# A graph network and a mixture of experts on one core: the experts' router turned round, and the gates' small operations spread over three engines

## The reference, cut to what matters

```
logits = xf @ Wr + br                    # 10000 x 8, xf = layernorm(x)
probs = softmax(logits); vals, idx = top_k(probs, 2)
cw = (one_hot(idx, 8) * vals[..., None]).sum(axis=1)
for e in range(8):                       # W1e 512 x 64, W2e 64 x 512
    h = relu(xf @ W1e + b1e)
    out += cw[:, e:e+1] * (h @ W2e + b2e)
x = x + out
```

## Time and profile before

| | |
|---|---|
| median of 3 runs | 2534.85 us |
| all runs | 2534.85, 2533.58, 3272.83 us |
| profiled execution, its own time | 2537.42 us |
| its span | 2535.6 us |
| mean granted clock of the profiled execution | 0.998 |
| busy over the span | PE 98%, DVE 74%, ACT 59%, POOL 44% |

### The profile page before, as it was taken

The page is one execution under the profiler, slowest core; times in us unless marked ns, Lnnn a source line. Parts: engine busy times, 40 slices in busy tenths (PEclk is TensorE's granted clock), DMA queues, the critical chain, the costliest instruction groups (busy, mean ns, idle before and its releaser), DMA issues.

```text
span 2535.6 us, 40119 instructions
## 1 busy us (share of the span) xinstructions
PE 2492.7 (98%) x9827; PEld 1624.6 (64%) x9827; DVE 1874.8 (74%) x4816; ACT 1491.9 (59%) x3550; POOL 1106.9 (44%) x1451
## 2 busy tenths in 40 slices
PE   8999999999999999999999999999999999999999
PEld 4444455555488874555558886555546888888887
DVE  5555565555599985555579996557748999999997
ACT  2222245555288875555548886555535666666665
POOL 3222245555144435555433333555534544444452
PEclk9999999999999999999999999999999999999999
DMA  5444468888355547888735555998852334533332
GB/s 149 133 133 133 130 201 265 272 266 271 96 166 165 163 162 254 273 263 273 248 96 166 164 165 188 337 335 271 271 184 80 103 106 137 168 117 93 105 102 70
DMA packets 208171, 460.89 MB, mean 182 GB/s; under 512 B 34896, under 2 KB 35208, under 8 KB 208005
## 3 DMA queue, kind: packets, MB, share of 16 engines
q0 software_dynamic: 64928, 207.55, 29.3%
q1 hardware_dynamic: 73812, 125.17, 14.1%
q10 hardware_dynamic: 69264, 126.12, 13.6%
HBM read 245.32 MB, written 213.93 MB: 181 GB/s over the span
## 4 chain that ended last, share of the span: by engine, by line
PE 79%; DVE 14%; issue 3%; DMA 1%; ACT 1%; POOL 0%; ACTq 0%; SPq 0%; DVEq 0%; POOLq 0%
PE psY L695 11%; PE psM L809 9%; PE psY L809 9%; PE psH L809 9%; PE psY L709 6%; PE psY L717 6%; PE psY L726 6%; PE psT L675 5%; PE psS L821 4%; PE psS L822 4%; DVE xls L1466 1%; DVE res L1554 1%; DVE res L1540 1%; DVE xcs L1469 1%; DVE rows L1530 1%
## 5 line engine op out<-in xcount | busy, mean ns | idle before, releaser
L566 POOL DMA_INDIRECT rows<-y_rows,lists x471 | 491.7, 1044 | 461.8 <-PE psS L822 339.8
L1359 DVE TENSOR_TENSOR lows<-rows,highs 128x512 fp32r<-128x512 f32 x471 | 325.8, 692 | 356.7 <-ACT highs L977 348.3
L977 ACT ACTIVATE outs<-psS 128x512 f32<-128x512 f32 x471 | 279.6, 594 | 272.2 <-PE psS L822 267.2
L977 ACT ACTIVATE highs<-rows 128x512 fp32r<-128x512 f32 x471 | 294.8, 626 | 147.2 <-ACT outs L977 107.1
L821 PE MATMUL psS<-highs,sel 128*128 128x512 f32 x471 | 346.9, 737 | 10.3 <-ACT outs L977 8.0
L573 POOL DMA_INDIRECT rows<-sum_rows,nodeI x158 | 211.2, 1337 | 313.8 <-DVE rows L1367 298.9
L695 PE MATMUL psY<-wy,res 128*128 128x512 f32 x632 | 286.7, 597 | 0.0
L977 ACT ACTIVATE outs<-psY 128x512 f32<-128x512 f32 x237 | 141.7, 599 | 231.2 <-PE psY L695 221.8
L809 PE MATMUL psM<-wz,res 128*128 128x512 f32 x544 | 255.6, 592 | 0.0
L809 PE MATMUL psY<-wz,res 128*128 128x512 f32 x536 | 251.7, 592 | 0.0
L809 PE MATMUL psH<-wz,res 128*128 128x512 f32 x528 | 248.0, 592 | 0.0
(11 more groups left out here) (201 smaller groups left out, 4893.2 us busy)
## 6 DMA issues: line engine op xcount, KB each, us to landing
sum_rows<-outs ACTq DMA_DIRECT2D x471, 256.0 KB, 3.7
y_rows<-outs SPq DMA_DIRECT2D x237, 256.0 KB, 2.0
rows<-in_x POOLq DMA_DIRECT2D x78, 256.0 KB, 3.2
outs<-in_x SPq DMA_DIRECT2D x78, 256.0 KB
out_rows<-res SPq DMA_DIRECT2D x78, 256.0 KB, 2.9
rows<-y_rows,lists POOLq DMA_INDIRECT x471, 4.3
z_rows<-res SPq DMA_DIRECT2D x13, 512.0 KB, 5.6
res<-z_rows SPq DMA_DIRECT2D x13, 512.0 KB, 4.5
```

The lines of the kernel that those rows point to most:

```text
L566: pool.indirect_dma_start(out=rows[:, t % RING, :], out_offset=None, in_=y_d, in_offset=bass.IndirectOffsetOnAxis(ap=col(srcT, t), axis=0) ...
L977: act.activation(o, i_, ACT.Copy).then_inc(signal, 1)
L1359: dve.tensor_tensor(lows[:, t % RING, :], rows[:, t % RING, :], highs[:, g, :].bitcast(F32), ALU.subtract)\
```

## The change

Five things change, all in the experts' stage.

1. The router's product is turned round: `wg2` (16 columns) is the stationary operand, and high and low part of the tile, now one tensor `x_both`, stream past together as 256 columns. Four matmuls take the place of eight, and the result is 16 x 256 in psM.
2. To have the logits by node again, ACT copies and negates that result to `logitT` (`take_logits`), and PE turns it with two 128 x 128 transposes after `up_parts` (`router_turn`).
3. DVE sums the four parts in one reduction over psM, ahead of `up_wide`; the bias's subtraction and the minimum stand each in front of a 512-column operation instead of waiting for one another.
4. The gates' high part goes from DVE to ACT (`gates_high`, behind `gated`), the low part from DVE to POOL (`gates_low`, first in POOL's iteration).
5. On POOL `scale_shift` stands ahead of `gather_own`. Some pairs of semaphores become one.

```diff
@@ POOL @@
+            def gates_low(k):
+                s = k % 2
+                high, low = (sm[:, s, a:a + 2 * X].rearrange("p (g e) -> p g e", g=2) for a in (HIGH, LOW))
+                pool.wait_ge(cw_high, k + 1)
+                pool.tensor_tensor(low, sm[:, s, CW:CW + X].unsqueeze(1).to_broadcast([P, 2, X]), high,
+                                   ALU.subtract).then_inc(cw_set[s], 1)
...
             for k in range(NT):
+                if k >= 1:
+                    gates_low(k - 1)
                 if k + 2 < NT:
                     negative_mean(k + 2)
                 gates(k)
+                if k + 2 < NT:
+                    scale_shift(k + 2)
                 if k + 4 < NT:
                     gather_own(k + 4, var_in, 1)
-                if k + 2 < NT:
-                    scale_shift(k + 2)
+            gates_low(NT - 1)
@@ PE @@
             def router(k):
...
+                pe.wait_ge(logit_set, k)
+                for q in range(C):
+                    mm = pe.matmul(psM[0:2 * X, 0:2 * P], wg2[:, q, :], x_both[:, :, s, q * P:(q + 1) * P],
+                                   start=(q == 0), stop=(q == C - 1))
+                mm.then_inc(router_ps, 1)
+
+            def router_turn(k):
+                s = k % 2
+                pe.wait_ge(logit_set, k + 1)
                 if k > 0:
                     pe.wait_ge(lg_sb[1 - s], (k - 1) // 2 + 1)
-                for q in range(C):
-                    pe.matmul(psM[:, 0:2 * X], xhs[:, s, q * P:(q + 1) * P], wg2[:, q, :], start=(q == 0), stop=False)
-                for q in range(C):
-                    mm = pe.matmul(psM[:, 0:2 * X], xls[:, s, q * P:(q + 1) * P], wg2[:, q, :], start=False,
-                                   stop=(q == C - 1))
-                mm.then_inc(lg_ps[s], 1)
+                for j in range(2):
+                    mm = pe.transpose(psM[:, (2 + j) * P:(3 + j) * P], logitT[:, j * P:(j + 1) * P], ident[:, :])
+                mm.then_inc(lg_ps, 1)
@@ ACT @@
+            def take_logits(k):
+                s, n = k % 2, k // 2
+                act.wait_ge(router_ps, k + 1)
+                act.wait_ge(lg_ps, k)
+                act.activation(logitT[0:2 * X, :], psM[0:2 * X, 0:2 * P], ACT.Copy, scale=-1.0).then_inc(logit_set, 1)
...
+            def gates_high(k):
+                s, n = k % 2, k // 2
+                act.wait_ge(cw_made, k + 1)
+                if k > 1:
+                    act.wait_ge(cw_ps, k - 1)
+                act.activation(sm[:, s, HIGH:HIGH + 2 * X].rearrange("p (g e) -> p g e", g=2).bitcast(F32R),
+                               sm[:, s, CW:CW + X].unsqueeze(1).to_broadcast([P, 2, X]), ACT.Copy).then_inc(cw_high, 1)
...
+                take_logits(k)
                 if k >= 1:
                     gated(k - 1)
+                    gates_high(k - 1)
@@ DVE @@
-                link(dve.tensor_copy(high.bitcast(F32R), twice))
-                dve.tensor_tensor(low, twice, high, ALU.subtract).then_inc(cw_set[s], 1)
...
                 if own:
+                    dve.wait_ge(lg_ps, k + 1)
+                    parts = psM[:, 2 * P:4 * P].rearrange("p (h r) -> p h r", h=2)[:, :, 0:2 * X]
+                    k_lg = step(dve.tensor_reduce(gate(LG), parts.rearrange("p h (g e) -> p e h g", g=2), AX.XY, ALU.add))
+                    up_wide(k)
                     after(k_lg)
-                    dve.tensor_reduce(stat(LOWEST), gate(LG), AX.X, ALU.min).then_inc(lg_sb[s], 1)
-                    up_wide(k)
+                    k_lg = step(dve.tensor_tensor(gate(LG), gate(LG), bgs[:, :], ALU.subtract))
```

More of the change, by code:

```diff
@@ L144, in build @@
         h_cross = nc.alloc_sbuf_tensor_at("h_cross", [P, D], F32R, offset=wz_at + 8 * D)
-        xhs = nc.alloc_sbuf_tensor_at("xhs", [P, 2, D], F32R, offset=wy_at)
-        xls = nc.alloc_sbuf_tensor_at("xls", [P, 2, D], F32R, offset=wy_at + 8 * D)
+        x_both = nc.alloc_sbuf_tensor_at("x_both", [P, 2, 2, D], F32R, offset=wy_at)
+        logitT = nc.alloc_sbuf_tensor_at("logitT", [P, 2 * P], F32, offset=wz_at + 12 * D)
+        xhs = x_both[:, 0]
+        xls = x_both[:, 1]
         xcs = nc.alloc_sbuf_tensor_at("xcs", [P, 2, D], F32R, offset=hw_at)
@@ L247, in build @@
         rstd_in = sems("rstd_in", 2)
-        shift_in = sems("shift_in", 2)
+        shift_in = sem("shift_in")
         oh_set = sems("oh_set", 4)
@@ L264, in build @@
         mend_st = sem("mend_st")
-        lg_ps = sems("lg_ps", 2)
+        lg_ps = sem("lg_ps")
         lg_sb = sems("lg_sb", 2)
-        p_sb = sems("p_sb", 2)
+        p_sb = sem("p_sb")
         cw_set = sems("cw_set", 2)
         hg_sb = sems("hg_sb", 2)
-        cw_ps = sems("cw_ps", 2)
+        cw_ps = sem("cw_ps")
+        cw_high = sem("cw_high")
         cw_sb = sems("cw_sb", 2)
@@ L288, in build @@
         pad_set = sem("pad_set")
+        router_ps = sem("router_ps")
+        logit_set = sem("logit_set")
         mean_in = sem("mean_in")
@@ L634, in scale_shift @@
                 pool.tensor_tensor(st[:, s, SHIFT:SHIFT + 1], st[:, s, MEAN:MEAN + 1], st[:, s, RSTD:RSTD + 1], ALU.mult)\
-                    .then_inc(shift_in[s], 1)
+                    .then_inc(shift_in, 1)
             def gates(k):
@@ L921, in hidden_turn @@
                 pe.transpose(psS[1][0:4 * X, 0:P], sm[:, s, HIGH:HIGH + 4 * X], ident[:, :])\
-                  .then_inc(cw_ps[s], 1)
+                  .then_inc(cw_ps, 1)
             def down_parts(k):
@@ L955, in _ @@
                 up_parts(k)
+                router_turn(k)
                 if k == 2:
@@ L1086, in exps @@
                                bias=st[:, s, LOWEST:LOWEST + 1], accum_out=st[:, s, SUM:SUM + 1])\
-                   .then_inc(p_sb[s], 1)
+                   .then_inc(p_sb, 1)
             def squares(k):
@@ L1104, in gated @@
                 g_.then_inc(hg_sb[s], 1)
+            def gates_high(k):
[5 more added lines that the diff above has]
+                               sm[:, s, CW:CW + X].unsqueeze(1).to_broadcast([P, 2, X]), ACT.Copy).then_inc(cw_high, 1)
             def norm(k):
                 s, n = k % 2, k // 2
-                act.wait_ge(shift_in[s], n + 1)
+                act.wait_ge(shift_in, k + 1)
                 act.activation(rows[:, 2 + s, :], kept(place(k)), ACT.Identity, scale=st[:, s, RSTD:RSTD + 1],
@@ L1117, in h_top @@
                 act.wait_ge(o_ps[s], n)
-                act.wait_ge(cw_ps[s], n + 1)
+                act.wait_ge(cw_ps, k + 1)
                 copy(cwT[0:4 * X, s, :], psS[1][0:4 * X, 0:P], cw_sb[s])
@@ L1145, in _ @@
             gated(NT - 1)
+            gates_high(NT - 1)
             widen_down(NT - 2)
@@ L1509, in gate @@
                     return sm[:, s, k:k + size]
[L1511 to L1516, removed]
                 if ahead:
@@ L1530, in experts @@
                     step(dve.scalar_tensor_tensor(v, a, 0.0, avec[:, :], ALU.min, ALU.mult))
+                if own:
+                    after(k_lg)
+                    dve.tensor_reduce(stat(LOWEST), gate(LG), AX.X, ALU.min).then_inc(lg_sb[s], 1)
+                if ahead:
                     dve.wait_ge(xe_in[s], 16 * (na + 1))
@@ L1533, in experts @@
                 if own:
-                    dve.wait_ge(p_sb[s], n + 1)
+                    dve.wait_ge(p_sb, k + 1)
                     step(dve.reciprocal(stat(INV), stat(SUM)))
@@ L1632, in _ @@
                     finish(k - 3)
-                if k >= 1:
-                    gate_parts(k - 1)
                 experts(k, ahead=(k + 2 < NT))
@@ L1639, in _ @@
             h_parts(NT - 2)
-            gate_parts(NT - 1)
             finish(NT - 2)
```

2 lines of the change are left out of this document (1 added, 1 removed).

## The result

The changed kernel takes 2517.78 us in the median (2517.22 to 2520.04, 5 runs). Its ratio to the kernel before is 0.9931, with a 95% interval of 0.9917 to 0.9946; run again later beside other kernels it was 0.9943 (0.9929 to 0.9957). The prediction said 2521 us, 0.55% faster, within 2513 to 2535. The interval does not reach 1, so the gain is clear of the noise, but it is under 2%, as the prediction had it with 0.96. The 3272.83 us among the runs of the kernel before is a slow execution; ratios compare fast ones alone.

A forecast was written before the change was run, and what follows sets the result against it. PE was taken to bound the kernel at 7.64 us an iteration, DVE next at 7.60. 76 x 0.18 us plus 0.5 once, less 0.2 in the drain, gave -14 us: median 2521 us, range 2513 to 2535.

The forecast's parts named there:

- PE led, by 0.04 us: Experts' stage before the change: PE sets the 7.64 us period, DVE alone needs about 7.60, read from its catching up early.
- PE's sum, -0.18 with ends -0.23 and +0.24: PE per iteration: old router -0.90, new router +0.50, two transposes +0.22 us, giving a period of 7.46 us.
- the margin around a stream: New router on PE: 0.017 us around each matmul's streaming time, so 0.124 us for 256 columns.
- DVE's need, 7.21: DVE per iteration after the change: 7.60 less 0.39 us for small operations removed or placed ahead of large ones.
- ACT and POOL hide what they are given: take_logits (0.35 us) and gates_high on ACT, gates_low (0.20 or twice that) on POOL: covered, costing nothing.
- The circle at 7.15 us: Logits' loop through PE, ACT and DVE back to the next router: 7.04 us, perhaps 0.1 more, under PE's 7.46.
- The reciprocal: DVE operation needing exps' sum: due 2.09 us after the reduction begins, just in time; otherwise some 0.1 us is added.
- -0.5 once for the late gather: POOL's moments ahead of the gather: norm no longer waits for a late gather, which once cost PE 0.5 us.
- The sum, -14 us: Whole profiled execution: 76 iterations at 0.18 us and 0.5 once, less 0.2 in the drain; 2537.4 to 2523.4 us.
- (a): Rival: the logits' circle or DVE leads at 7.46 to 7.64 us; 2521 to 2535 us; chance 0.19 together with (c).
- (b): Rival: new router's four matmuls charged as plain float32, 0.86 to 0.92 us; time 2553 us; chance 0.06.
- (c): Rival: PE gets its 0.18 but DVE keeps 7.60 us; 3 us gained, 2531; chance 0.19 together with (a).

The follow-up runs named there:

- e2: The kernel before with only the gates' split moved, high part to ACT and low part to POOL: 2535.02 us, ratio to before 0.9998.
- e5: The changed kernel with router_turn's two transposes made twice: 2536.51 us, ratio to before 1.0001.
- e6: The changed kernel with two of up_parts' four low matmuls left out: 2498.79 us, ratio to before 0.9854.
- e3: The changed kernel with the gates' split back on DVE: 2522.11 us, ratio to before 0.9942.
- e1: The kernel before with only POOL's order changed, scale_shift ahead of gather_own: 2536.09 us, ratio to before 0.9997.
- e4: The changed kernel with POOL's old order, the gather ahead of scale_shift: 2522.86 us, ratio to before 0.9946.
- e9: The changed kernel run again without any edit: 2520.13 us, ratio to before 0.9943.
- e7: The changed kernel with the bias's subtraction and the minimum directly behind the reduction, ahead of up_wide: 2521.24 us, ratio to before 0.9940.
- e8: The changed kernel with high and low part added in psum by eight 128-column router matmuls, leaving one transpose: 2516.36 us, ratio to before 0.9924.
- e11: The changed kernel with the activation's slope as one constant in experts' ahead part, a one-source DVE operation: 2519.18 us, one execution, no ratio.

## Why the prediction was right, point by point

**PE led, by 0.04 us.** That PE led is right: e2 takes work off DVE in the kernel before and gets nothing, and in the changed kernel e5 adds two transposes to PE and gets 0.233 us. The 0.04 rests on the one stretch of the prediction; no run tested it by itself.

**PE's sum, -0.18 with ends -0.23 and +0.24.** Measured -0.20. The transposes were 0.23 (0.22 taken) and the four wide matmuls 0.47 (0.50 taken), 0.117 each instead of 0.124, so that the old router's 0.90 closes the sum. The term that was mis-sized is the margin around a stream: I took 0.017 us from the 512-column group, and it is 0.010 with 16 columns of weights. The Trainium skill's rule ("TensorE: Matmul & The Clock Gate", "Back-to-back issue gap"), columns / 2.4 + 2.5 ns, gives 0.109; the page states it for a single matmul, without its weight load, which the prediction did not say. The trace's 0.117 lies between it and my value.

**DVE's need, 7.21.** Right: 7.207 in e6, and 7.50 in e3, which by the same sum would be 7.21 + 0.31 = 7.52.

**ACT and POOL hide what they are given.** Right for ACT: take_logits took 0.375 us (0.35 taken), gates_high 0.199 (0.20) and norm 0.802 (0.80), the turn's copy was there in time, and PE never waited. gates_low took 0.61 us where I had 0.20 to 0.40, and it is hidden all the same.

**The circle at 7.15 us.** Not seen, since DVE's 7.21 lies over it; e6 shows that it is not longer. The reciprocal did not wait.

**-0.5 once for the late gather.** 0.65, shown by e1 (gone) and e4 (back, 0.85). That POOL's order is worth another 0.025 us an iteration in the changed kernel I did not foresee.

**The sum, -14 us.** The profiles are 17.8 apart. Of the missing 3.8, 1.3 are the router's (75 x 0.200 against 13.7), 0.15 the late iteration, 0.5 the drain and the time ahead of the first router, which got shorter and not longer, and 1.8 the first three iterations, probably most of it the clock. The change itself is worth 15.5 to 16 us, by those executions and by the medians of e9 and of the kernel before beside it (2520.13 and 2536.22). So the mechanism was right and the size some 10% low.

**The rivals.** (a) fell with e6. (b), the price of plain float32, fell with 0.117 us a matmul. (c), DVE keeps 7.60, fell with e6 and e3 (its time, 2535 less 3, is 2532 and not 2531); but a part of the gain does hang on DVE's relief, as e3 shows.

## What to carry to other kernels

When two engines stand full, find out which leads from the stretches where one catches up, and count what the other needs alone: here they lay 0.04 us apart by that reading. DVE's relief alone gained nothing (e2), PE's relief with only a part of DVE's stopped at 7.50 us (e3), and the gates' move, worth nothing by itself, was worth 4 us together with the router. A product with few output columns is a candidate for having these columns as the stationary side, since the cost is then the columns streamed and not eight full weight loads, even if the result has to be turned back: here 0.47 and 0.23 us against 0.90. In a chain of small DVE operations each link costs 0.19 to 0.22 us (e7); placed singly in front of large ones with nothing to wait for, each costs 0.07 to 0.08.

## What the runs showed of the hardware that I had not expected

**The price of a matmul with 16 columns of weights.** Start to start: 0.117 us for 256 columns and 0.060 for 128, where 16 columns against 128 columns of weights cost 0.112. So the weight load of 128 columns sets the small ones' pace, and with 16 columns of weights it is gone.

**POOL and DVE exclude each other while DVE works on two operands in sbuf.** (psum is where PE leaves its products, sbuf the memory of the other tiles.) gates_low (128 x 16) takes 0.21 us in e2, where, in the timeline of both engines, it starts as L1532 has ended and ends before L1504, which reads psum, begins some 0.1 us later:

```profile
2207.11 0.75 DVE L1532 SCALAR_TENSOR_TENSOR rows<-rows,rdeg,res 128x512 f32<-128x512 f32 x1
...
2207.87 0.21 POOL L658 TENSOR_TENSOR sm<-sm 128x16 f32<-128x16 f32 x1
...
2208.17 0.70 DVE L1504 SCALAR_TENSOR_TENSOR psY<-psY,res 128x512 f32<-128x512 f32 x1 [0.24 <-PE psY L911]
```

In the changed kernel it starts at 2210.85 and ends at 2211.46, just behind L1558 (2210.70 to 2211.38), which reads rows and avec, both in sbuf. POOL's timeline of the changed kernel:

```profile
2208.67 0.19 POOL L639 TENSOR_TENSOR st<-st 128x1 f32<-128x1 f32 x1
2209.38 1.43 POOL L620 DMA_INDIRECT rows<-sum_rows,nodeI  x1 [0.52 <-issue]
2210.85 0.61 POOL L662 TENSOR_TENSOR sm<-sm 128x16 f32<-128x16 f32 x1
```

The other runs moved its start, and the end stayed with DVE's. It starts 0.14 us into L1558 in the changed kernel and takes 0.61, 0.17 into it in e8 (L1559 there) and takes 0.59, 0.37 into it in e6 and takes 0.39: each time it ends 0.07 to 0.08 us behind the DVE operation. Beside up_wide, which reads psum, it takes 0.22 to 0.23 (e4, e7). In e5 its start drifts across the start of L1558, and there the two change places. Two iterations of e5, POOL's and DVE's timelines:

```profile
2004.01 0.23 POOL L662 TENSOR_TENSOR sm<-sm 128x16 f32<-128x16 f32 x1
2004.04 0.76 DVE L1558 SCALAR_TENSOR_TENSOR rows<-rows,avec 128x512 f32<-128x512 f32 x1
...
2011.70 0.78 POOL L662 TENSOR_TENSOR sm<-sm 128x16 f32<-128x16 f32 x1
2011.72 0.69 DVE L1558 SCALAR_TENSOR_TENSOR rows<-rows,avec 128x512 f32<-128x512 f32 x1
```

With POOL 0.03 us ahead, POOL takes its own time and DVE's operation is 0.07 longer; with POOL 0.02 ahead, DVE takes its own time and POOL's operation is 0.55 longer. Over 2000 to 2400 us, 37 iterations of e5 are of the first kind (0.23 to 0.25 us for gates_low) and the other 15 have 0.75 to 0.78. So the wait goes both ways, and the small operation has more to lose.

The gather's issue takes 1.16 us elsewhere. Started 0.34 us into L1546 (rows and res) it takes 1.43, started 0.14 into it in e6 1.64, and it ends 1.03 us behind L1546 both times. Started within 0.03 us of the DVE operation's start, it takes 1.15 to 1.16 (e1, e7), so it is not every phase of the issue that is held. The operation L639, 0.19 us beside a psum-reading DVE operation here, took 0.55 us in the kernel before, where it stood beside L1521 (rows and res).

The Trainium skill, "Advanced Engine Details and Errata", section "Mode Summary", notes that the second Vector port to sbuf is shared with GpSimd and speaks of DVE's two-port modes; its section "GPSIMD Details" adds DVE instructions with two sbuf inputs, and these rows agree with that for float32 operations with two sources at 0.68 us for 512 columns. That the port is the cause was not shown by an experiment, since e11 moved the phases.
